# A mixture-of-experts layer after graph attention: scaled expert rows are added to the residual in the output by an accumulating scatter, in place of a last combining stage

## The reference, cut to what matters

```python
x = x + gnn(layernorm(x), adj, W, a)      # x: (16, 512, 128) f32, graph attention with 4 heads
x = x + ffn(layernorm(x), Wg, bg, W1, b1, W2, b2)

def ffn(x, ...):                          # E = 8 experts, K = 2 of them for each token
    gate_scores = einsum('bsd,ed->bse', x, Wg) + bg
    topk_scores, topk_idx = top_k(gate_scores, K)
    topk_probs = softmax(topk_scores)
    combine = sum(topk_probs[..., None] * one_hot(topk_idx, E), axis=-2)
    out = 0
    for e in range(E):
        h = relu(einsum('bsd,hd->bsh', x, W1[e]) + b1[e])      # hidden 512
        y = einsum('bsh,dh->bsd', h, W2[e]) + b2[e]            # back to 128
        out = out + combine[..., e:e + 1] * y
    return out
```

## Time and profile before

| | |
|---|---|
| median of 3 runs | 709.22 us (705.26 to 709.45) |
| the profiled execution | 703.93 us |
| its span, first to last instruction | 702.1 us |
| busy in the span: PE / DVE / ACT / POOL | 72% / 78% / 64% / 64% |
| last landing of a scatter of the first stage | about 421.0 us into the span |
| last landing of a scatter of the expert stage | about 652.9 us |
| mean granted TensorE clock | 0.855 of full |

### The profile page before, as it was taken

The page is one execution under the profiler, slowest core; times in us unless marked ns, Lnnn a source line. Parts: engine busy times, 40 slices in busy tenths (PEclk is TensorE's granted clock), DMA queues, the critical chain, the costliest instruction groups (busy, mean ns, idle before and its releaser), DMA issues.

```text
span 702.1 us, 23589 instructions
## 1 busy us (share of the span) xinstructions
PE 505.2 (72%) x7510; PEld 461.2 (66%) x7570; DVE 546.9 (78%) x1573; ACT 450.1 (64%) x916; POOL 448.9 (64%) x404
## 2 busy tenths in 40 slices
PE   0457998788777888788884208999999999996000
PEld 0345987687777887778783106888888888885000
DVE  2756899988999999999987524878888888785465
ACT  0348798686767676576662106888888888883343
POOL 0012454888787888888888770877878787777100
PEclk9975999988988878888987557999999999999555
DMA  7911121322211222212001152333333333330687
GB/s 245 382 38 61 63 63 63 92 82 92 84 49 69 86 79 83 66 47 87 31 29 39 40 116 55 94 84 90 90 87 86 90 86 93 84 89 25 212 254 252
DMA packets 62059, 67.67 MB, mean 96 GB/s; under 512 B 7122, under 2 KB 45693, under 8 KB 61968
## 3 DMA queue, kind: packets, MB, share of 16 engines
q1 hardware_dynamic: 43616, 44.31, 21.2%
q0 software_dynamic: 8816, 17.46, 7.8%
q10 hardware_dynamic: 9536, 4.73, 2.4%
HBM read 44.16 MB, written 23.22 MB: 96 GB/s over the span
## 4 chain that ended last, share of the span: by engine, by line
issue 33%; DVE 25%; POOL 19%; DMA 9%; ACT 5%; PE 4%; DVEq 2%; SPq 1%; POOLq 1%; another core or an unknown queue 0%; ACTq 0%
POOL expert_out L492 12%; POOL expert_rows L444 5%; DMA adji<-expert_out 3%; DVE bs L710 3%; DVE rowt L926 3%; ACT G L517 2%; DVE G L733 2%; DMA out<-adji 2%; DMA G<-in_L_ffn_W 2%; DMA expert_rows<-rowt,idx 2%; DVE mv L713 1%; DVE T L742 1%; DVE s L801 1%; ACT xn L522 1%; PE bank L1150 1%
## 5 line engine op out<-in xcount | busy, mean ns | idle before, releaser
L492 POOL DMA_INDIRECT expert_out<-ysb,bidx x142 | 170.5, 1200 | 61.5 <-issue 43.1
L444 POOL DMA_INDIRECT expert_rows<-rowt,idx x128 | 145.3, 1135 | 45.3 <-issue 31.9
L517 ACT ACTIVATE G<-bank,s2c 128x512 uint8<-128x512 f32 x256 | 154.5, 700 | 21.4 <-remote 21.4
L1150 PE MATMUL bank<-V,G 128*128 128x66 bf16 x3072 | 135.5, 201 | 31.8 <-ACT G L517 28.2
L609 ACT ACTIVATE G<-bank,b1s,sc 128x256 f32<-128x256 f32 x284 | 137.2, 563 | 12.8 <-PE bank L1310 12.8
L1150 PEld LDWEIGHTS bank<-V,G 128*128 128x128 fp8e4 x3072 | 126.0, 102 | 9.6 <-issue 3.2
L1320 PE MATMUL bank<-W2h,G 128*128 x1704 | 106.5, 219 | 2.8 <-DVE ysb L1075 1.3
L1320 PEld LDWEIGHTS bank<-W2h,G 128*128 128x128 f16 x1704 | 96.5, 97 | 18.1 <-issue 17.8
L1310 PE MATMUL bank<-xt,W1h 128*128 128x256 f16 x852 | 106.9, 276 | 0.0
L1060 DVE TENSOR_TENSOR G<-G 128x1024 f16<-128x1024 f32 x71 | 87.0, 1225 | 2.4
L1310 PEld LDWEIGHTS bank<-xt,W1h 128*128 x852 | 81.5, 99 | 9.1
(11 more groups left out here) (158 smaller groups left out, 867.9 us busy)
## 6 DMA issues: line engine op xcount, KB each, us to landing
adji<-in_adj SPq DMA_DIRECT2D x16, 1024.0 KB, 5.8
xb<-expert_rows SPq DMA_DIRECT2D x71, 130.0 KB
adji<-expert_out SPq DMA_DIRECT2D x16, 512.0 KB, 4.5
out<-adji ACTq DMA_DIRECT2D x16, 256.0 KB, 3.1
expert_out<-ysb,bidx POOLq DMA_INDIRECT x142
G<-in_L_ffn_W SPq DMA_DIRECT2D x1, 2048.0 KB, 14.3
expert_rows<-rowt,idx POOLq DMA_INDIRECT x128, 2.4
xr<-in_x SPq DMA_DIRECT2D x1, 768.0 KB, 10.6
```

Source lines behind the costliest of these rows:

```text
L444: pool.indirect_dma_start(xs, bass.IndirectOffsetOnAxis(ap=idx[:, Z.p, k, j:j + 1], axis=0), rowt[:, Z.p, j, :], None).then_inc(scattered[ ...
L492: pool.indirect_dma_start(ybuf, bass.IndirectOffsetOnAxis(ap=bidx[:, B.o, t:t + 1], axis=0), ysb[:, B.q, t, :], None, bounds_check=2 * TOK ...
L517: act.activation(Gs[:, M.p, h // 2, mt, :, h % 2], zb[h][:, :], ACT.Sign, bias=s2c[:, M.p, mt, h:h + 1]).then_inc(S["z_used"], 1)
L1150: last = mm(o[:, h, :], G8[:, R.p, h // 2, mt, nt * P:(nt + 1) * P, h % 2], v[:, h, :], start=False, stop=(part == H and mt == NT - 1 and ...
```

## The change

The last stage goes, and with it `expert_out`, `PR`, the loads L400, the work of L620, L1084 and L1090 and the stores L625. In its place:

- SP stores x1 to the output during the first stage, batch by batch, from six batches behind the loads of the adjacency matrices.
- The scattered rows are two words longer: they carry both probabilities. Their target is the token's row itself.
- DVE works out in the expert stage, for each block, which probability belongs to this expert (`wk`, `wt`), and multiplies the scaled result by it (a second pass over `ysb`).
- POOL's scatter adds its rows to the output (`compute_op=ALU.add`).
- A token's two rows lie in blocks of two different experts, so the first scatter of an expert waits until all blocks of the experts before it have landed: the table gets a third row with that number, POOL reads it with `value_load`, and SP announces the landings in order (`announce`, semaphore `landed`), that of block n-6 after it has issued the load of block n.

```diff
-ROW = D + 2
+ROW = D + 4
...
+            def store_x1(R):
+                sp.wait_ge(S["x1_ready"], R.n * 2 + 2)
+                sp.dma_start(outd[:, bass.ds(R.n * NT, NT), :], xr[:, bass.ds(R.n * NT, NT), :]) \
+                  .then_inc(S["x1_stored"], 16)
...
             def load_rows(B):
                 ge(sp, S["bt_ready"], B.n - 3)
-                ge(sp, S["bidx_ready"], B.n - 3)
+                ge(sp, S["w_steps"], (B.n - 3) * 3 - 1)
...
+            def announce(B):
+
+                sp.wait_ge(back[B.q], 16 * BT * (B.f + 1))
+                sp.sem_inc(S["landed"], 1)
+
+            LAG = 6
+            for n in range(BLOCKS):
+                load_rows(Batch(n))
+                if n >= LAG:
+                    announce(Batch(n - LAG))
+            for n in range(BLOCKS - LAG, BLOCKS):
+                announce(Batch(n))
...
             def send(B):
+
+                first = pool.value_load(tab[0:1, 2, bass.ds(B.n, 1)], min_val=1, max_val=BLOCKS)
                 hold(pool, S["bidx_ready"], B.n + 1, S["pool_turns"])
                 hold(pool, S["y_ready"], B.n + 1, S["pool_turns"])
+                hold(pool, S["landed"], first, S["pool_turns"])
                 for t in range(BT):
                     pool.indirect_dma_start(
-                        ybuf, bass.IndirectOffsetOnAxis(ap=bidx[:, B.o, t:t + 1], axis=0),
-                        ysb[:, B.q, t, :], None, bounds_check=2 * TOK - 1, oob_is_err=False) \
+                        outr, bass.IndirectOffsetOnAxis(ap=bidx[:, B.o, t:t + 1], axis=0),
+                        ysb[:, B.q, t, :], None, bounds_check=TOK - 1, oob_is_err=False, compute_op=ALU.add) \
                         .then_inc(back[B.q], 16)
...
-                    dve.scalar_tensor_tensor(bidx[:, U.o, :], xb[:, U.q, :, D + 1], tf[:, 5, bass.ds(U.n, 1)],
-                                             xb[:, U.q, :, D], ALU.not_equal, ALU.add).then_inc(S["bidx_ready"], 1)
+                    dve.tensor_copy(bidx[:, U.o, :], xb[:, U.q, :, D]).then_inc(S["bidx_ready"], 1)
+                    c = Chain(dve, S["w_steps"], 3, U.n)
+                    here = tf[:, 5, bass.ds(U.n, 1)]
+                    c.did(dve.scalar_tensor_tensor(wk[:, U.p, 0, :], xb[:, U.q, :, D + 1], here, xb[:, U.q, :, D + 2],
+                                                   ALU.is_equal, ALU.mult))
+                    c.did(dve.scalar_tensor_tensor(wk[:, U.p, 1, :], xb[:, U.q, :, D + 1], here, xb[:, U.q, :, D + 3],
+                                                   ALU.not_equal, ALU.mult))
                     split(U)
+                    c.wait()
+                    c.did(dve.tensor_tensor(wt[:, U.q, :], wk[:, U.p, 0, :], wk[:, U.p, 1, :], ALU.add))
...
                     dve.scalar_tensor_tensor(ysb[:, Y.q], Yp[Y.p], sc[:, 11:12],
                                              b2b[:, bass.ds(ex, 1), :].to_broadcast([P, BT, D]),
-                                             ALU.mult, ALU.add).then_inc(S["y_ready"], 1)
+                                             ALU.mult, ALU.add).then_inc(S["y_steps"], 1)
+                    dve.wait_ge(S["w_steps"], Y.n * 3 + 3)
+                    dve.wait_ge(S["y_steps"], Y.n + 1)
+                    dve.tensor_tensor(ysb[:, Y.q], ysb[:, Y.q], wt[:, Y.q, :].unsqueeze(2).to_broadcast([P, BT, D]),
+                                      ALU.mult).then_inc(S["y_ready"], 1)
```

More of the change, by code:

```diff
@@ L211, in build @@
         den = sb("den", [P, NT])
-        PR = sb("PR", [P, 2, TILES])
         pos = sb("pos", [P, NT, E])
@@ L371, in _ @@
             sp.dma_start(xr[:, XSPLIT:TILES, :], xd[:, XSPLIT:TILES, :]).then_inc(S["ld_x1"], 16)
-            with sp.Fori(0, (NB - 2) // 2) as i:
-                load_adj(Batch(2, i))
-                load_adj(Batch(3, i))
+            def store_x1(R):
+                sp.wait_ge(S["x1_ready"], R.n * 2 + 2)
+                sp.dma_start(outd[:, bass.ds(R.n * NT, NT), :], xr[:, bass.ds(R.n * NT, NT), :]) \
+                  .then_inc(S["x1_stored"], 16)
+            AHEAD = 6
+            for n in range(2, AHEAD):
+                load_adj(Batch(n))
+            with sp.Fori(0, (NB - AHEAD) // 2) as i:
+                for u in range(2):
+                    load_adj(Batch(AHEAD + u, i))
+                    store_x1(Batch(u, i))
+            for n in range(NB - AHEAD, NB):
+                store_x1(Batch(n))
             pad_rows(sp, range(E // 2))
@@ L614, in _ @@
             steps(act, hidden)
-            def first(n, q, k):
-                act.wait_ge(ld_y[k], q * 16 + 16)
-                for j in range(NT):
-                    act.activation(yin[:, k, j, 0, :], yin[:, k, j, 0, :], ACT.Copy,
-                                   scale=PR[:, 0, bass.ds(n * NT + j, 1)]).then_inc(S["first_ready"], 1)
-            def store(n, k):
-                act.wait_ge(S["final_ready"], n + 1)
-                act.dma_start(outd[:, bass.ds(n * NT, NT), :], yin[:, k, :, 1, :]).then_inc(stored[k], 16)
[L626 to L629, removed]
-            with act.Fori(1, 4) as q:
-                for k in range(4):
-                    first(q * 4 + k, q, k)
-                    store(q * 4 + k - 1, (k - 1) % 4)
-            store(15, 3)
         @block.vector
@@ L1049, in _ @@
             step(dve.tensor_scalar(tab[:, 1, :], tf[:, 0, :], float(E - 1), None, ALU.min))
+            step(dve.tensor_scalar(tab[:, 2, :], tf[:, 1, :], 1.0, None, ALU.add))
             step(dve.tensor_scalar(tf[:, 5, :], tf[:, 0, :], -1.0, float(E), ALU.mult, ALU.add))
```

44 lines of the change are left out of this document (15 added, 29 removed).

## The result

The changed kernel takes 761.55 us (755.36 to 765.81, 4 runs), the kernel before 708.72 us in the runs beside it: a ratio of 1.0744, 95% interval 1.0701 to 1.0787. The forecast was 717, the range 689 to 744. The profiled execution took 761.23 us, its span is 759.4 us.

A forecast was written before the change was run, and what follows sets the result against it. PE and POOL were taken to pace the expert stage, then a new loop through the landing: 70 blocks at 3.64 us from 436.44, plus tail and changes of expert, replacing the 49.25 us last stage: span 709.8, median 717, range 689 to 744.

The forecast's parts named there:

- the paragraph on the accumulating scatter: Expert stage: the add lengthens each POOL indirect DMA (0.98 us) by 0.1 and the landing by 0.8, 1.0 in the loop.
- the part on the loop: Expert stage: load s+7 waits for block s's landing; 13.57 us per four blocks, 3.39 each; with the add 14.57, 3.64.
- Rival 3: Expert stage: POOL becomes the bound at 1.47 us a DMA, 4.0 a block; span 735, median 742; chance 0.13 with the clock.
- The page: Scatter transfer: the skill gives an in-flight add half the copy's rate, doubling the transfer and possibly read descriptors, as in Rival 3.
- The landing: Scatter's start to its landing in the expert stage: 2.2 us plain, 0.8 more with the add, at most 2.15 more.
- rival 1: Expert stage: accumulating scatter as quick as a plain one, 3.39 us a block; span 686.7, median 694; chance 0.33.
- Changes of expert: Eight times POOL holds a scatter until earlier ones land: 8 x 1.8 x 0.8 = 11.7 us; 7 with a plain landing.
- The first stage and the stores of x1: First stage: SP's stores of x1, rows 16 bytes longer and the table's extra step cost nothing.
- DVE: Expert stage: DVE's work a block grows from 2.40 to 3.16 us, slightly above today's pace but not the bound.
- rival 4: Expert stage: PE's clock falls to 1.2 GHz for a tenth of 250 us, adding about 10 us; chance 0.13 with Rival 3.

The follow-up runs named there:

- open_plain: Changed kernel with a plain scatter in place of the accumulating one (LAG 6, two passes), on an undisturbed chip: 710.78 us, 1.0056 of the kernel before.
- e1_plain: Changed kernel with a plain scatter in place of the accumulating one, the same kernel as open_plain on another chip: 717.02 us, 1.0144 of the kernel before.
- v1_half_rows: Kernel before with `expert_out` and `ysb` in 16-bit floats, last-stage loads waiting only for their buffer's use: 695.11 us, 0.9818 of the kernel before.
- open_lag8: Changed kernel with a plain scatter and LAG 8 in place of 6, on an undisturbed chip: 683.07 us, 0.9657 of the kernel before.
- e2_before_add: Kernel before with compute_op=add on its scatter and first-stage stores of x1 to add to: 789.59 us, 1.1186 of the kernel before.
- e3_lag8: Changed kernel, accumulating scatter kept, with LAG 8 in place of 6: 763.81 us, 1.0799 of the kernel before.
- open_lag8_onepass: Changed kernel with plain scatter, LAG 8, and without DVE's weights and second pass, on an undisturbed chip: 677.74 us, 0.9572 of the kernel before.

## Why the prediction was wrong

**The step that failed** is in the paragraph on the accumulating scatter: "POOL's 0.98 may stay (lower bound) or grow by half [...] I take 0.1 each". It grew by 0.57 us at the least (0.98 to 1.55) in each of two instructions a block, above even the upper bound (0.49), and stands at 1.72 in the mean. By itself this undoes the premise of the part on the loop, that "POOL then has some slack": 2 x (1.72 + 0.29) = 4.02 us a block is more than the 3.64 of the loop. I had named 1.2 us for POOL's instruction as the point at which the prediction is wrong; it is at 1.72. It was the value nearest to a row of a plain scatter, taken for an instruction of which no row showed anything.

**Rival 3 had the right mechanism and was undersized.** It gave 4.0 us a block and a span of 735. Measured against 759.4: the start 2.9 us later; 70 x 4.34 = 303.8 in place of 280 + 12, so 11.8; and a tail of 15.6 in place of 6, so 9.6. I had counted the wait before the empty blocks among the eight changes, but not that all eight DMAs of these blocks queue up behind it. Together 24.3 us. Its chance, 0.13 with the clock, was too small, and the range ended at 744 because of it.

**The page.** In the expert stage the packets of POOL's queue take 3.8 times as long with the add (94.6 us against 25.0) for the same 8.4 MB, and are 4.5 times as many (20448 against 4544). The Trainium skill (Collectives: The Full Stack, "The bandwidth ceiling: the fold count and why AG ≠ RS ≠ AR") gives half the copy's rate for an add on the way. Taken as twice the time, this is in the direction of the trace but short of it, and the measurement decides. It was not what cost the time: the DMA engines stay at 0.45. What cost it was POOL's time to issue, of which that page says nothing.

**The landing** was sized about rightly as a difference. I added 0.8 us; the medians are 3.42 with the add and 2.83 or 2.33 without (open_plain, e1_plain), so 0.6 to 1.1 apart. The base of 2.2, from one row each, was too small by 0.1 to 0.6 us, and the load of the rows took 2.33 to 2.51 instead of 2.15.

**The loop** was right as a mechanism, as LAG 8 shows in the plain kernel (27.7 us), and it is not what bounds the kernel with the add, as LAG 8 shows there (nothing gained). Its price without the add was too small: rival 1 has a span of 686.7 and open_plain's is 709.5. Of the 22.8 us, 0.6 are its start, 262.4 - 244.3 = 18.1 the blocks (3.75 with the changes of expert, against 3.39 + 0.10) and 4.2 the tail (10.1 against 5.9). Landing and load, 0.63 and 0.36 above the rows that I took, would make 1.0 in the loop, 0.25 a block or 17 us. But in e1_plain the same reckoning gives 0.13 + 0.18 = 0.31, 5 us, and its blocks take 3.77 all the same. The other candidate is the order of experts, for which I had 7 us where POOL waits 26.0 us (open_plain) and 19.8 us (e1_plain) for it. Which of them makes up the 18.1 is not shown.

**Changes of expert.** I had 11.7 us. The trace after has 24.4 us of POOL waiting for SP's announcement in 13 waits, and without the order the kernel is 10.8 us quicker (761.55 to 750.76, on two chips; the intervals of the two ratios lie apart). That is near the predicted size by luck: I had POOL start late in a stage where it has slack. It has none, so all 24.4 us are its own time, and more than half of them are lost again because its DMAs grow in the mean when nothing holds them (1.72 to 1.81, 13 us over 142).

**The first stage and the stores of x1** at nothing: right, 1.0016 (0.9983 to 1.0049), though the rows are 8 bytes longer, two words, and not 16. The 2.9 us by which the changed kernel's expert stage begins later are within what profiles of equal first stages differ by: the first result comes at 437.0 us in open_plain and at 439.0 in e1_plain, which are one kernel, and at 443.4 in v1_half_rows, whose first stage is that of the kernel before (436.4).

**DVE**: 3.16 forecast, 3.23 seen where it is the bound (open_lag8). It is no bound in the changed kernel (70 of 100 us).

**The clock.** The granted clock was 0.91 in the stretch shown, so the lower level (1.2 GHz) did come for a part of it, as rival 4 says. It is not the cause: e2_before_add and e3_lag8 have 0.97 and 0.96 in the same stretch, at 4.06 and 4.37 us a block.

**Left open**: what the order of experts costs the plain kernel on an undisturbed chip (POOL waits 24.5 us for it in open_lag8_onepass, but no run takes it away), and what the second pass adds to POOL's time beside L1048.

## What to carry to other kernels

A change that adds an operation of which the trace has no row should first be priced at the engine that issues it, not only at its transfer: here an add in a DMA cost that engine 0.57 us for 128 rows, on a queue that had no slack. Where a load comes to stand behind a completion, the sum from one to the other over the number of blocks between them gives the pace, and the distance (here 6 or 8) is the cheap cure. A last stage bound by its bytes may be worth more made smaller (-1.8%) than moved into a stage in which the engine that has to do more is full (+7.4%). The move itself was not the loss: with a plain scatter, which leaves out the sum, and LAG 8 the kernel was 3.4% quicker than before.

## What was not expected of the hardware

- An indirect DMA of 128 rows of 512 bytes takes POOL at least 0.977 us, and 1.551 us if it accumulates. The accumulating one shows 144 packets in place of 32, and its packets take 3.8 times the DMA engines' time.
- An accumulating one of which all 128 rows lie out of bounds takes POOL 1.55 us all the same.
- Beyond 0.98 and 1.55 us it grows beside DVE's instruction with two inputs of 128x1024 (up to 1.97 and 2.31 us), and less beside one of 128x256 (up to 1.57 in the changed kernel, 1.80 in e3_lag8).
- POOL's time for it does not depend on the bytes of a row: 1.199 us in the mean with 256 bytes a row, 1.200 with 512, for 128 rows.
- PE can stand still inside a row of matmuls for 1.2 us with no wait that the trace shows; this made 31.9 us in one run of a kernel and 3.1 us in its run on another chip. On two of the chips the kernel before took 776 and 779 us in place of 708.
